# The last stage of a four-layer graph network: one PSUM bank per chunk, twice x as an early float32 product, the last norm on two engines

## The chip, the core and the metric

The kernel runs on one core of a Trainium2 chip. The core has five engines that run their own instruction streams and meet only at semaphores: TensorE (matrix products, into PSUM), VectorE, ScalarE, GpSimd and SyncE (which issues DMAs). The time is the device time of one execution in microseconds. Before the change it was 1755.76 us (median of 3 runs, 1755.16 to 1755.86).

## The reference

Node states x (3125 nodes, 128 features) go through four layers of a graph network over 100,000 edges, each followed by `x = layernorm(x + layer(x))`. The change concerns the end of the fourth, a graph isomorphism layer:

```python
def _L3_gnn_ref(x, edge_index, W, b, gamma, beta, gin_eps):
    agg = jax.ops.segment_sum(x[src], dst, num_segments=x.shape[0])
    h = (1.0 + gin_eps[0]) * x + agg
    h = h @ W.T + b
    mean = jnp.mean(h, axis=0)                     # over the nodes
    var = jnp.mean(jnp.square(h - mean), axis=0)
    h = gamma * (h - mean) * jax.lax.rsqrt(var + BN_EPS) + beta
    return jax.nn.relu(h) + x
...
x = _layernorm(x + _L3_gnn_ref(x, ...), axis=-1)   # so: layernorm(relu(bn(z)) + 2 x)
return x
```

The batch norm needs the statistics of all nodes, so nothing of Relu or the last norm can start until the last node's z = h W^T + b is known. Behind it come Relu, the sum with 2x, and a norm over the 128 features of each node.

## The kernel before

The nodes stand in 25 tiles of 128 (the last holds 53), in `CHUNKS` of four tiles (seven chunks, the last of one tile) or in `PAIR`s of eight (three pairs and one tile). The edges are turned into a dense adjacency matrix `adj` in SBUF, with which every layer's sum over neighbours is a matrix product; x is split for it into three bf16 parts, `parts[0..2]`, whose sum is x in float32. A long loop over the edges (layer 1) fills most of the time; layers 2 and 3 follow. The order of the work is written out by hand for every engine, and each engine runs its list in order.

The end of layer 3: for each chunk u, `l3_terms` sums into PSUM bank u (the tail into bank 7), VectorE copies the sum to SBUF (`l3_out`, into `acc`), TensorE multiplies it by the weight back into the same bank (`l3_linear`, signals `gin_ready`), ScalarE adds the bias and writes z, with features on partitions, to `agg_all` (`gin_rows`, signals `gin_out`), and VectorE takes batch statistics of it (`zt_stats`). `agg_all` and `xn`, which holds x in float32 by rows, are the same 3200 columns of the arena: from here on x exists only as its three parts. VectorE then forms scale and bias of the batch norm as two columns of `cols`, with ScalarE's square root (`root`) in between. At `phase_end(eng, 8)` each engine drains, adds one to `phase_ends` and waits for all five.

The last stage runs over the four groups of `PAIR`. ScalarE applies Relu with scale and bias to eight tiles of z at once (`bn_relu`). TensorE, for every tile, adds twice x into PSUM as three bf16 products of `parts` with `ident_h` (an identity that VectorE doubles just then) and adds the Relu's tile, turned by a float32 product with `ident_f` (`fin_ready`); it has two banks for a group and two groups in flight, so from the third group on it waits for `out_ready`. VectorE's `layernorm` takes statistics of each of the eight rows of tiles, combines them, lets ScalarE take the roots, forms the reciprocal and normalises eight times, from PSUM into `xn`. SyncE stores a group when it is done. The branch `If_ne(flag, 0)` serves graphs that don't fit the fast layout; it isn't taken here.

Of the kernel before, what the change touches and what calls it, by code (L numbers as in the profile page):

```python
# [23 lines left out]
ALU = mybir.AluOpType  # L24
ACT = mybir.ActivationFunctionType

P = 128
N = 3125
E = 100000
D = 128  # L30
# [13 lines left out]
CH = 4  # L44
# [26 lines left out]
def build(nc, t, out, x1_d, xa_d, xb_d, table_d, late_d):  # L71
    ctx = ExitStack()
    with ctx:
# [3 lines left out]
        def sem(name):  # L77
            return ctx.enter_context(nc.semaphore(name))
# [111 lines left out]
        agg_all = arena[:, 4800:8000]  # L190


        eps_i = late[:, 0:P]
        node2 = [late[:, P + 512 * u:P + 512 * (u + 1)].rearrange("p (j d) -> p j d", d=D) for u in range(2)]


# [25 lines left out]
        cnt_ready = sem("cnt_ready")  # L222
        adj_written = sem("adj_written")
        lin_base = {0: 0, 1: NC, 2: 3 * NC}
        zero_ready = sem("zero_ready")
        deg_ready = sem("deg_ready")
        words_moved = sem("words_moved")
        c1_sum_ready = sem("c1_sum_ready")
# [55 lines left out]
        fin_ready = sem("fin_ready")  # L284
        out_ready = sem("out_ready")
        twice_ready = sem("twice_ready")
        out_stored = sem("out_stored")
        off_ready = sem("off_ready")
        off_t = sem("off_t")
# [103 lines left out]
        def dst_bank(u):  # L393
            return ps[:, u, :] if u < NC - 1 else ps[:, 7, P:2 * P]
# [64 lines left out]
        def _(sp):  # L459
# [188 lines left out]
            with sp.Else():  # L648
# [7 lines left out]
                sp.wait_ge(xb_ready, NC)  # L656
                l2_affine()
                sp.sem_inc(phase_ends, 1)
            phase_end(sp, 8)

            for g, (k0, nt) in enumerate(PAIR):
                sp.wait_ge(out_ready, g + 1)
                if nt == 2 * CH:
                    sp.dma_start(out[k0 * P:(k0 + nt) * P, :].rearrange("(k p) d -> p k d", p=P),
                                 xn[:, k0:k0 + nt, :]).then_inc(out_stored, 16)
                else:
                    sp.dma_start(out[k0 * P:N, :], xn[0:TAIL, k0, :]).then_inc(out_stored, 16)
# [4 lines left out]
        def _(pool):  # L672
# [100 lines left out]
            with pool.Else():  # L773
# [3 lines left out]
                    pool.tensor_tensor(xn[:, k0:k0 + nt, :], xn[:, k0:k0 + nt, :], over(beta_b, nt), ALU.add  # L777
                                       ).then_inc(xb_ready, 1)
                pool.sem_inc(phase_ends, 1)
            phase_end(pool, 8)  # L780


        @block.tensor
        def _(pe):
# [447 lines left out]
            with pe.If_ne(flag, 0):  # L1232
                pe.wait_ge(update_loaded, 48)
                pe.wait_ge(bn_loaded, 16)
                for c in range(NC):
                    update(c)
                transposed_weight(loads[7], 16)
                scan(pe, X2, scan_tile)
                layer(2, gcn, summed, peeled=2)
                phase_end(pe, 7)  # L1240
                transposed_weight(loads[9], 80)
                scan(pe, X3, scan_tile)
                layer(3, gin, summed, peeled=1)
            with pe.Else():
                for c, bank in ((NC - 2, 6), (NC - 1, 3)):
                    update_tiles(c, range(CHUNKS[c][1]), bank, w_b)
                behind = late_sums(EARLY - 1)
                for u in behind:
                    l2_terms(EARLY - 1, u, True, False)
                weight_t(loads[7], 16, 0)  # L1250
                weight_t(loads[9], 80, 1)
                pe.wait_ge(low_ready, 2 * NC + NC - 1)
                for u in range(NC):
                    if u == 2:
                        pe.wait_ge(wt_ready, 2)
                    if u == 3:
                        pe.wait_ge(lin_used, 3 * NC)
                    l2_terms(NC - 2, u, u not in behind, False)
                pe.wait_ge(low_ready, 3 * NC)
                for u in ORDER:  # L1260
                    l2_terms(NC - 1, u, False, True)
                l2_linear(ORDER[0])
                l2_linear(ORDER[1])
                pe.wait_ge(eps_ready, 1)
                for n, c in enumerate(ORDER[:-1]):
                    pe.wait_ge(low_ready, 3 * NC + n + 1)
                    for u in ORDER:
                        if n == 0:
                            pe.wait_ge(agg_out, 2 * NC + AT[u] + 1)
                        l3_terms(c, u)  # L1270
                    if n + 2 < NC:
                        l2_linear(ORDER[n + 2])
                pe.wait_ge(low_ready, 4 * NC)
                pe.wait_ge(wt_ready, 2)
                for u in range(NC):
                    l3_terms(ORDER[-1], u)
                    if u:
                        l3_linear(u - 1)
                l3_linear(NC - 1)
                pe.sem_inc(phase_ends, 1)  # L1280
            phase_end(pe, 8)

            pe.wait_ge(twice_ready, 1)
            for g, (k0, nt) in enumerate(PAIR):
                pe.wait_ge(bn_relu, g + 1)
                if g >= 2:
                    pe.wait_ge(out_ready, g - 1)
                for j in range(nt):
                    k = k0 + j
                    o = ps[:, 2 * (g % 2) + j // CH, (j % CH) * D:(j % CH + 1) * D]  # L1290
                    for q in range(3):
                        pe.matmul(o, ident_h[:, :], parts[q][:, k, :], start=(q == 0), stop=False)
                    last = pe.matmul(o, agg_all[:, k * P:(k + 1) * P], ident_f[:, :], start=False, stop=True)
                last.then_inc(fin_ready, 1)


        @block.scalar
        def _(act):
# [1 line left out]
                out = words(k0, k1).bitcast(F32)  # L1300
                act.activation(out, cols[:, 6:7].broadcast_to([P, (k1 - k0) * NP // 2]), ACT.Copy)

            act.wait_ge(zero_ready, 1)
            zero(3, 8)
            for n in range(8):
                half, a = n // 4, n % 4
# [280 lines left out]

            def gin_chunk(c, k0, nt):
                act.wait_ge(gin_ready, c + 1)
                act.activation(agg_all[:, k0 * P:(k0 + nt) * P], ps[:, 4, 0:nt * P], ACT.Identity,  # L1590
                               bias=cols[:, 0:1]).then_inc(gin_out, 1)

            def two_roots(c, k0, nt):
# [54 lines left out]
            def gin_rows(u):  # L1648
                k0, nt = CHUNKS[u]
                act.wait_ge(gin_ready, u + 1)  # L1650
                act.activation(agg_all[:, k0 * P:(k0 + nt) * P], dst_bank(u), ACT.Identity,
                               bias=cols[:, 0:1]).then_inc(gin_out, 1)

            with act.Else():
# [22 lines left out]
                root(1)  # L1677
                act.sem_inc(phase_ends, 1)
            assert roots[0] == after
            phase_end(act, 8)  # L1680

            for k0, nt in PAIR:
                act.activation(agg_all[:, k0 * P:(k0 + nt) * P], agg_all[:, k0 * P:(k0 + nt) * P], ACT.Relu,
                               bias=cols[:, 6:7], scale=cols[:, 5:6]).then_inc(bn_relu, 1)
            for k0, nt in PAIR:
                root(nt)


        @block.vector
        def _(dve):  # L1690
            own = Count(dve, v_own)

            dve.memset(cols[:, 7:8], EPS)
            dve.memset(cols[:, 6:7], 0.0).then_inc(zero_ready, 1)
            own.add(dve.memset(off[:, :], 0.0))
            dve.wait_ge(loads[0], 48)
            own.add(dve.tensor_scalar(hi_i[0:GRP, :], raw_src[0:GRP, :], 7, None, ALU.arith_shift_right))
# [498 lines left out]
            def zt_stats(c):  # L2196
                k0, nt = CHUNKS[c]
                dve.wait_ge(gin_out, c + 1)
                w = nt * P if nt == CH else TAIL
                own.add(dve.bn_stats(stats[:, c, :], agg_all[:, k0 * P:k0 * P + w]))  # L2200

            def gcn_all(add, rows, ahead):
                added = [0]
# [18 lines left out]
            with dve.If_ne(flag, 0):  # L2222
# [17 lines left out]
                for c in range(NC):  # L2240
                    add_self(3, c, gin_ready, 0)
                    zt_stats(c)
                own.wait()
                dve.sem_inc(var_ready, ROOTS)
                roots[0] += ROOTS
                dve.sem_inc(v_own, OWN_MORE)
# [70 lines left out]
            with dve.Else():  # L2317
# [12 lines left out]
                for c in ORDER:  # L2330
# [14 lines left out]
                    if c == ORDER[0]:  # L2345
                        add_sums(ORDER[5])
                        add_sums(ORDER[6])
                dve.wait_ge(loads[9], 80)
                for u in range(NC):
                    l3_out(u)  # L2350
                    if u:
                        zt_stats(u - 1)
# [10 lines left out]
            own.wait()  # L2363
            own.add(dve.tensor_tensor(rstd[:, 1:2], cols[:, 5:6], mv[:, 0, 0:1], ALU.mult))
            own.wait()
            dve.tensor_tensor(cols[:, 6:7], cols[:, 2:3], rstd[:, 1:2], ALU.subtract)
            phase_end(dve, 8)

            dve.tensor_scalar(ident_h[:, :], ident_h[:, :], 2.0, None, ALU.mult).then_inc(twice_ready, 1)
            for g, (k0, nt) in enumerate(PAIR):  # L2370
                dve.wait_ge(fin_ready, g + 1)
                b = 2 * (g % 2)
                layernorm(ps[:, b:b + 2, :].rearrange("p a (j d) -> p (a j) d", d=D), xn[:, k0:k0 + nt, :], nt, done=out_ready)


_INS = ["x", "src", "dst", "edge_attr_64", "L0_gnn_W_self1", "L0_gnn_W_neigh1", "L0_gnn_b1", "L0_gnn_W_self2",
# [26 lines left out]
```

## Time and profile before

| | us |
|---|---|
| median of the runs shown | 1755.76 |
| the profiled execution, its own time | 1752.44 |
| its span, first to last instruction | 1750.3 |
| TensorE busy in the span | 1468.5 |
| VectorE busy | 760.0 |
| ScalarE busy | 668.9 |
| last product of layer 3 ends, from the span's start | 1718.46 |
| last store issued | 1746.60 |

The profiled execution's own time contains a little beyond the span. Times in the rows below count from the span's start. Busy shares over the whole span say nothing of the last stage, which is 2% of it; it has to be read from its own chain and timeline. PE is TensorE's matmul unit and PEld its weight load, DVE is VectorE, ACT ScalarE, SPq the DMA queue of SyncE. A float32 product appears as two instructions of PE.

### The profile page before, as it was taken

Reading aid. Unit: us, or ns where it says so; the run is one execution under the profiler, and the core shown is the slowest. Engines: PE = TensorE matmul, PEld = TensorE weight load, DVE = VectorE, ACT = ScalarE, POOL = GpSimd, SP = SyncE. Lnnn points to the kernel's source line nnn. Section 1 sums busy time; section 2 is a strip of 40 time slices with the busy share of each in tenths; the row PEclk is TensorE's granted clock in tenths of the full one; section 3 lists DMA queues with packets and bytes.
Section 4 is the critical chain, followed back from the end, with each engine's and each line's share of the span. In section 5 each row is a group of like instructions: output and inputs, shape, how many; then the busy total and the mean of one; then the engine's idle time right before and its main releaser. Section 6 shows DMA issues by size and latency. Waiting matters only on the chain.

```text
span 1750.3 us, 31633 instructions
## 1 busy us (share of the span) xinstructions
PE 1468.5 (84%) x9759; PEld 1049.2 (60%) x9872; DVE 760.0 (43%) x2792; ACT 668.9 (38%) x1236; POOL 784.7 (45%) x819
## 2 busy tenths in 40 slices
PE   1789999969986877888888888889888988957996
PEld 1346666644545766676666666667666766634554
DVE  6997888622333322233334334323433343235445
ACT  3765555520002433344335334434433453321111
POOL 4300000000003777777777777777777777710000
PEclk9999999989997999989999999999999999969998
DMA  2000000001005333333333333333333333300001
GB/s 78 1 0 1 2 1 1 2 25 38 0 0 158 98 82 82 82 86 83 82 80 87 83 82 80 88 79 85 84 82 82 83 86 82 74 11 1 1 1 38
DMA packets 158697, 95.81 MB, mean 55 GB/s; under 512 B 120584, under 2 KB 143879, under 8 KB 158607
## 3 DMA queue, kind: packets, MB, share of 16 engines
q0 software_dynamic: 25088, 51.43, 11.4%
q1 hardware_dynamic: 133519, 43.21, 10.0%
q8 instruction: 53, 0.87, 0.2%
q14 instruction: 37, 0.30, 0.1%
HBM read 87.24 MB, written 7.32 MB: 54 GB/s over the span
## 4 chain that ended last, share of the span: by engine, by line
PE 31%; DMA 11%; POOL 9%; issue 8%; DVE 5%; ACT 2%; DVEq 2%; SPq 1%; POOLq 0%; ACTq 0%
DMA arena<-x_w1a,idx 9%; POOL arena L751 9%; PE ps L1077 6%; PE ps L1217 6%; PE ps L1086 5%; PE ps L1070 4%; PE ps L1058 3%; PE ps L1066 3%; PE ps L1127 1%; PE ps L1201 1%; DVE arena L1986 1%; DVEq L328 1%; DMA arena<-in_edge_attr 1%; DVE idx L1955 1%; ACT arena L1490 1%
## 5 line engine op out<-in xcount | busy, mean ns | idle before, releaser
L751 POOL DMA_INDIRECT arena<-x_w1a,idx x784 | 742.3, 947 | 692.2 <-issue 651.9
L1480 ACT ACTIVATE arena<-ps 88x512 f32<-88x512 f32 x196 | 116.3, 594 | 478.9 <-PE ps L1058 473.4
L1086 PEld LDWEIGHTS ps<-arena 128*128 128x128 f32 x1568 | 208.4, 195 | 111.5 <-issue 74.0
L1066 PE MATMUL ps<-ident_f,arena 128*128 128x128 f32 x784 | 132.6, 294 | 110.4 <-DMA arena<-x_w1a,idx 109.7
L1986 DVE TENSOR_TENSOR arena<-ps,bias_b 128x512 f32<-128x512 f32 x196 | 135.6, 692 | 204.6 <-PE ps L1077 204.6
L1981 DVE TENSOR_TENSOR arena<-win_i,late 128x96 f32<-128x96 f32 x196 | 51.4, 262 | 391.5 <-PE ps L1086 380.7
L1077 PE MATMUL ps<-w_c,arena 128*128 128x128 f32 x1568 | 221.3, 287 | 0.0
L1319 ACT ACTIVATE adj<-ps 128x300 f32 x392 | 172.5, 450 | 125.2 <-PE ps L815 118.1
L1070 PE MATMUL ps<-arena 88*128 88x512 f32 x392 | 208.3, 613 | 3.7 <-ACT arena L1480 3.7
L1077 PEld LDWEIGHTS ps<-w_c,arena 128*128 128x128 f32 x1568 | 204.4, 203 | 0.2
L1086 PE MATMUL ps<-arena 128*128 128x24 f32 x1568 | 197.0, 264 | 5.3 <-ACT arena L1490 2.9
L810 PE MATMUL ps<-arena 128*128 128x300 bf16 x784 | 168.2, 297 | 34.4 <-DVE arena L1754 30.4
L1754 DVE TENSOR_SCALAR arena<-late,arena 128x300 bf16<-128x300 int16 x784 | 191.6, 309 | 0.0
L1066 PEld LDWEIGHTS ps<-ident_f,arena 128*128 128x128 f32 x784 | 91.1, 148 | 163.9 <-DMA arena<-x_w1a,idx 158.7
L1486 ACT ACTIVATE arena<-ps,cols 128x512 f32<-128x512 f32 x196 | 134.7, 687 | 73.0 <-PE ps L1077 73.0
L1058 PE MATMUL ps<-ident_f,arena 128*88 128x128 f32 x784 | 128.1, 289 | 21.8 <-DMA arena<-in_edge_attr 14.6
L810 PEld LDWEIGHTS ps<-arena 128*128 128x128 bf16 x784 | 83.5, 115 | 91.6 <-DVE arena L1754 38.9
L827 PE MATMUL ps<-adj,arena 128*128 128x512 bf16 (+1 forms) x498 | 134.5, 357 | 0.5 <-issue 0.2
L1490 ACT ACTIVATE arena<-arena 128x512 f32<-128x512 f32 x196 | 123.4, 630 | 10.5 <-DVE arena L1986 3.3
L815 PE MATMUL ps<-adj,ident_h 128*128 x392 | 124.0, 316 | 0.8 <-ACT adj L1319 0.2
L959 PE MATMUL ps<-adj,arena 128*128 (+1 forms) x513 | 104.0, 362 | 16.6 <-DVE arena L1813 16.1
L1217 PE MATMUL ps<-adj,arena 128*128 128x512 bf16 (+1 forms) x513 | 108.2, 363 | 8.8 <-DVE arena L2309 4.8
(187 smaller groups left out, 1447.0 us busy)
## 6 DMA issues: line engine op xcount, KB each, us to landing
arena<-in_edge_attr SPq DMA_DIRECT2D x196, 128.0 KB, 2.5
arena<-x_w1a,idx POOLq DMA_INDIRECT x784
arena<-x_w1b SPq DMA_DIRECT2D x196, 12.0 KB
x_spill<-arena SPq DMA_DIRECT2D x1, 1600.0 KB, 7.2
x_w1a<-arena SPq DMA_DIRECT2D x6, 256.0 KB, 2.3
x_w1b<-arena SPq DMA_DIRECT2D x6, 256.0 KB, 2.6
arena<-x_spill SPq DMA_DIRECT2D x6, 256.0 KB, 2.8
out_x<-arena SPq DMA_DIRECT2D x3, 512.0 KB
```

Of the source, the lines that this page charges most:

```text
L751: pool.indirect_dma_start(out=z_e[v][:, j * D:(j + 1) * D], out_offset=None, in_=xa_d[:, :], in_offset=bass.IndirectOffsetOnAxis(ap=idx[:, ...
L810: last = pe.matmul(ps[:, bank, 0:NT * WIN_A], oh_src[v][:, :, j], oh_dst[v][:, j, :], start=(j == 2 * h), stop=False)
L1058: last = pe.transpose(ps[0:KE, 0, j * P:(j + 1) * P], ec[v % 2][:, j, :], ident_f[:, :])
L1066: pe.matmul(z_t[:, j * P:(j + 1) * P], z_e[v][:, j * P:(j + 1) * P], ident_f[:, :], is_transpose=True, start=(j == 0), stop=False)
L1070: pe.matmul(z_t, w_e[v % 2][0:KE, :], ec_t[0:KE, :], start=False, stop=True).then_inc(z_ready[v], 1)
L1077: last = pe.matmul(ps[:, 5, j * P:(j + 1) * P], h_t[:, j * P:(j + 1) * P], w_c[:, :], start=True, stop=True)
L1086: last = pe.matmul(ps[:, WIN_BANK[v % 2], 0:WIN], msg[:, j * P:(j + 1) * P], oh_e[v][:, j, :], start=(j == 0), stop=(j == J - 1))
L1217: last = pe.matmul(dst_bank(u), parts[q][:, k, :], adj[:, k, k0 * P:(k0 + nt) * P], start=((k, q) == (NT - 1, 0)), stop=(u != NC - 2 and ( ...
L1319: act.activation(adj[:, :, bass.ds(b, WIN_A)], ps[:, q % 4, 0:NT * WIN_A].rearrange("p (k w) -> p k w", w=WIN_A), ACT.Copy).then_inc(adj_w ...
L1490: act.activation(msg, msg, ACT.Relu).then_inc(msg_ready[v], 1)
L1754: last = dve.tensor_scalar(oh_dst[v][:, j, :], iota_c, comb[:, bass.ds(s, 1), j], None, ALU.is_equal)
L1986: dve.tensor_tensor(msg.rearrange("p (j d) -> p j d", d=D), bank(5, J), over(bias_b, J), ALU.add).then_inc(m_sum[v], 1)
```

## The change

- z goes to `z_t`, which is `acc`, the place of the sums it is made from, and not over `xn`: x stays whole in float32.
- Twice x is one float32 product for a chunk, 512 columns of `xn` against `twice_i`, a doubled identity that VectorE now makes ahead of its layer-3 copies. It opens the accumulation in PSUM bank c of chunk c. Four chunks' products stand ahead of the first Relu's tiles in TensorE's order, the others between the chunks.
- Relu goes by chunks of four tiles, and TensorE adds each chunk's four tiles to its bank. With a bank for every chunk, nothing in TensorE's list waits for `out_ready`.
- The join of all engines, `phase_end(eng, 8)`, is gone. ScalarE waits for VectorE's factors by `cols_ready`.
- VectorE takes statistics by chunk. In a group of eight tiles it normalises the first four and ScalarE the other four, with the negated scaled mean `nbias` as bias. VectorE's combining of the next group's statistics waits until both halves are done, since they read the same `mv`, `rstd` and `nbias`.

```diff
+        z_t = acc
+        twice_i = late[:, 9 * P:10 * P]
...
-            phase_end(sp, 8)
-
             for g, (k0, nt) in enumerate(PAIR):
-                sp.wait_ge(out_ready, g + 1)
+                sp.wait_ge(out_ready, min(2 * g + 2, NC))
...
-            phase_end(pe, 8)
-
             pe.wait_ge(twice_ready, 1)
-            for g, (k0, nt) in enumerate(PAIR):
-                pe.wait_ge(bn_relu, g + 1)
-                if g >= 2:
-                    pe.wait_ge(out_ready, g - 1)
+
+            def twice_x(c):
+                k0, nt = CHUNKS[c]
+                pe.wait_ge(gin_out, c + 1)
+                pe.matmul(ps[:, c, 0:nt * D], twice_i, xn[:, k0:k0 + nt, :].rearrange("p k d -> p (k d)"),
+                          start=True, stop=False)
+
+            def add_bn(c):
+                k0, nt = CHUNKS[c]
+                pe.wait_ge(bn_relu, c + 1)
                 for j in range(nt):
-                    k = k0 + j
-                    o = ps[:, 2 * (g % 2) + j // CH, (j % CH) * D:(j % CH + 1) * D]
-                    for q in range(3):
-                        pe.matmul(o, ident_h[:, :], parts[q][:, k, :], start=(q == 0), stop=False)
-                    last = pe.matmul(o, agg_all[:, k * P:(k + 1) * P], ident_f[:, :], start=False, stop=True)
+                    last = pe.matmul(ps[:, c, j * D:(j + 1) * D], z_t[:, (k0 + j) * P:(k0 + j + 1) * P], ident_f[:, :],
+                                     start=False, stop=(j == nt - 1))
                 last.then_inc(fin_ready, 1)
+
+            for c in range(4):
+                twice_x(c)
+            for c in range(NC):
+                add_bn(c)
+                if c + 4 < NC:
+                    twice_x(c + 4)
...
-            phase_end(act, 8)
-
-            for k0, nt in PAIR:
-                act.activation(agg_all[:, k0 * P:(k0 + nt) * P], agg_all[:, k0 * P:(k0 + nt) * P], ACT.Relu,
+            act.wait_ge(cols_ready, 2)
+            for k0, nt in CHUNKS:
+                act.activation(z_t[:, k0 * P:(k0 + nt) * P], z_t[:, k0 * P:(k0 + nt) * P], ACT.Relu,
                                bias=cols[:, 6:7], scale=cols[:, 5:6]).then_inc(bn_relu, 1)
-            for k0, nt in PAIR:
+            for g, (k0, nt) in enumerate(PAIR):
                 root(nt)
+                if nt == 2 * CH:
+                    act.wait_ge(fin_norm, g + 1)
+                    for j in range(CH, nt):
+                        last = act.activation(xn[:, k0 + j, :], ps[:, 2 * g + 1, (j - CH) * D:(j - CH + 1) * D], ACT.Identity,
+                                              scale=rstd[:, j:j + 1], bias=nbias[:, j:j + 1])
+                    last.then_inc(out_ready, 1)
...
                 dve.wait_ge(loads[9], 80)
+                dve.tensor_scalar(twice_i, ident_f[:, :], 2.0, None, ALU.mult).then_inc(twice_ready, 1)
                 for u in range(NC):
                     l3_out(u)
...
-            phase_end(dve, 8)
-
-            dve.tensor_scalar(ident_h[:, :], ident_h[:, :], 2.0, None, ALU.mult).then_inc(twice_ready, 1)
...
             for g, (k0, nt) in enumerate(PAIR):
-                dve.wait_ge(fin_ready, g + 1)
-                b = 2 * (g % 2)
-                layernorm(ps[:, b:b + 2, :].rearrange("p a (j d) -> p (a j) d", d=D), xn[:, k0:k0 + nt, :], nt, done=out_ready)
+                halves = [(2 * g, CH), (2 * g + 1, CH)] if nt == 2 * CH else [(2 * g, nt)]
+                for c, n in halves:
+                    dve.wait_ge(fin_ready, c + 1)
+                    for j in range(n):
+                        own.add(dve.bn_stats(stats[:, CH * (c - 2 * g) + j, :], rows_of(c, n)[:, j, :]))
+                own.wait()
+                if g:
+                    dve.wait_ge(out_ready, 2 * g)
+                for j in range(nt):
+                    last = dve.bn_aggr(mv[:, j, :], stats[:, j, :])
+                last.then_inc(var_ready, 1)
...
+                if nt == 2 * CH:
+                    dve.scalar_tensor_tensor(out=nbias[:, 0:nt], in0=mv[:, 0:nt, 0], scalar=-1.0, in1=rstd[:, 0:nt],
+                                             op0=ALU.mult, op1=ALU.mult).then_inc(fin_norm, 1)
+                c, n = halves[0]
+                for j in range(n):
+                    last = dve.tensor_scalar(xn[:, k0 + j, :], rows_of(c, n)[:, j, :], mv[:, j, 0:1], rstd[:, j:j + 1],
+                                             ALU.subtract, ALU.mult)
```

How the lists of the engines read before and after, with the semaphores that each row waits for. TensorE, from the last product of layer 3 on (`ps` is PSUM, `arena` holds z, x and its parts). Before:

```order
L1229 MATMUL ps<-arena,w_a 128x128 [waits agg_out]
L1244 UNCONDITIONAL_BRANCH
L1292 MATMUL ps<-arena,ident_h 128x128 [waits bn_relu,twice_ready,phase_ends]
L1292 MATMUL ps<-arena,ident_h 128x128 x2
L1293 MATMUL ps<-ident_f,arena 128x128
L1292 MATMUL ps<-arena,ident_h 128x128 x3
L1293 MATMUL ps<-ident_f,arena 128x128
```

In the changed kernel, at the same place (`late` holds the doubled identity):

```order
L1229 MATMUL ps<-arena,w_a 128x128 [waits agg_out]
L1245 UNCONDITIONAL_BRANCH
L1287 MATMUL ps<-arena,late 128x512 [waits gin_out,twice_ready]
L1287 MATMUL ps<-arena,late 128x512 [waits gin_out] x3
L1294 MATMUL ps<-ident_f,arena 128x128 [waits bn_relu]
L1294 MATMUL ps<-ident_f,arena 128x128 x3
L1287 MATMUL ps<-arena,late 128x512 [waits gin_out]
L1294 MATMUL ps<-ident_f,arena 128x128 [waits bn_relu]
L1294 MATMUL ps<-ident_f,arena 128x128 x3
```

The first instruction that needs the Relu was the first of the stage; now it is the fifth, behind four products that need only x.

VectorE, one group of eight tiles of the last norm. Before (the second group):

```order
L1838 BN_STATS stats<-ps 128x6 [waits fin_ready,v_own]
L1838 BN_STATS stats<-ps 128x6 x7
L1841 BN_AGGR mv<-stats 128x2 [waits v_own]
L1841 BN_AGGR mv<-stats 128x2 x7
L1845 RECIPROCAL rstd<-std 128x8 [waits std_ready]
L1848 TENSOR_SCALAR arena<-ps,mv,rstd 128x128 [waits v_own]
L1848 TENSOR_SCALAR arena<-ps,mv,rstd 128x128 x7
```

In the changed kernel, the same group:

```order
L2392 BN_STATS stats<-ps 128x6 [waits fin_ready]
L2392 BN_STATS stats<-ps 128x6 x3
L2392 BN_STATS stats<-ps 128x6 [waits fin_ready]
L2392 BN_STATS stats<-ps 128x6 x3
L2397 BN_AGGR mv<-stats 128x2 [waits out_ready,v_own]
L2397 BN_AGGR mv<-stats 128x2 x7
L2401 RECIPROCAL rstd<-std 128x8 [waits std_ready]
L2404 SCALAR_TENSOR_TENSOR nbias<-mv,rstd 128x8 [waits v_own]
L2408 TENSOR_SCALAR arena<-ps,mv,rstd 128x128 x4
```

Four of the eight normalising instructions have left VectorE; the combining has a new wait for the other engine's half of the group before.

ScalarE, from the root of the batch norm on. Before:

```order
L1405 ACTIVATE std<-mv,cols 128x1 [waits var_ready]
L1654 UNCONDITIONAL_BRANCH
L1683 ACTIVATE arena<-arena,cols 128x1024 [waits phase_ends]
L1683 ACTIVATE arena<-arena,cols 128x1024 x2
L1683 ACTIVATE arena<-arena,cols 128x128
L1405 ACTIVATE std<-mv,cols 128x8 [waits var_ready] x3
L1405 ACTIVATE std<-mv,cols 128x1 [waits var_ready]
```

In the changed kernel:

```order
L1414 ACTIVATE std<-mv,cols 128x1 [waits var_ready]
L1663 UNCONDITIONAL_BRANCH
L1691 ACTIVATE arena<-arena,cols 128x512 [waits cols_ready]
L1691 ACTIVATE arena<-arena,cols 128x512 x5
L1691 ACTIVATE arena<-arena,cols 128x128
L1414 ACTIVATE std<-mv,cols 128x8 [waits var_ready]
L1698 ACTIVATE arena<-ps,nbias,rstd 128x128 [waits fin_norm]
L1698 ACTIVATE arena<-ps,nbias,rstd 128x128 x3
L1414 ACTIVATE std<-mv,cols 128x8 [waits var_ready]
```

Between the roots stand now four normalising instructions a group, read from PSUM.

## Rows read from the trace of the kernel before

**Rows 1.** Chain that ended last: start us, us, what (x instructions)
```profile
1704.18 0.86 PE ps L1229 x2
...
1720.85 0.16 DVE cols L2366
...
1721.08 1.25 ACT arena L1683
...
1722.46 0.48 PE ps L1292 x3
1722.94 0.53 PE ps L1293 x2
...
1728.15 0.29 PE ps L1293 x2
1728.46 1.70 DVE stats L1838 x8
```

**Rows 2.** Timeline of the last norm: start us, us, engine, line, instruction, [idle before]
```profile
1733.99 1.68 DVE L1838 BATCH_NORM_STATS2 stats<-ps 128x6 f32<-128x128 f32 x8
...
1735.70 0.64 DVE L1841 BATCH_NORM_AGGREGATE mv<-stats 128x2 f32<-128x6 f32 x8
...
1736.38 0.30 ACT L1405 ACTIVATE std<-mv,cols 128x8 f32<-128x8 f32 x1 [5.22 <-DVE mv L1841]
...
1736.71 0.20 DVE L1845 RECIPROCAL rstd<-std 128x8 f32<-128x8 f32 x1 [0.37 <-ACT std L1405]
...
1736.95 2.64 DVE L1848 TENSOR_SCALAR arena<-ps,mv,rstd 128x128 f32<-128x128 f32 x8
...
1739.57 1.68 DVE L1838 BATCH_NORM_STATS2 stats<-ps 128x6 f32<-128x128 f32 x8
...
1745.42 0.18 DVE L1841 BATCH_NORM_AGGREGATE mv<-stats 128x2 f32<-128x6 f32 x1
...
1746.60 0.26 SPq L667 DMA_DIRECT2D out_x<-arena  x1
```

**Rows 3.** Waits of SyncE's queue: who for whom, us in total, times, longest
```profile
SPq L73 <- DMA out_x<-arena: 3.0, 1, 3.0
```

**Rows 4.** Timeline of TensorE, layers 2 and 3
```profile
1677.40 1.05 PE L1181 MATMUL ps<-w_c,arena 128*128 128x128 f32 x8
...
1716.78 1.68 PE L1229 MATMUL ps<-arena,w_a 128*128 128x512 f32 x4
```

**Rows 5.** Timeline of a layer-2 norm that both engines write
```profile
1684.80 0.30 ACT L1405 ACTIVATE std<-mv,cols 128x4 f32<-128x4 f32 x1 [3.53 <-DVE mv L2003]
1685.13 0.18 DVE L2288 RECIPROCAL rstd<-std 128x4 f32<-128x4 f32 x1 [0.36 <-ACT std L1405]
...
1685.42 1.11 DVE L2296 TENSOR_SCALAR arena<-late,mv,rstd 128x128 f32<-128x128 f32 x4
1685.54 1.65 ACT L1639 ACTIVATE arena<-late,nbias,rstd 128x128 bf16<-128x128 f32 x4 [0.44 <-DVE nbias L2290]
```

**Rows 6.** ScalarE by form: shapes, count | busy us, mean ns
```profile
L1683 ACT ACTIVATE arena<-arena,cols 128x1024 f32<-128x1024 f32 x3 | 3.5, 1231 | 0.8 <-DVEq L306 0.8
...
L1301 ACT ACT_TABLE_LOAD x1 | 1.3, 1283 | 0.6 <-PEq L2388 0.6
...
L1683 ACT ACTIVATE arena<-arena,cols 128x128 f32<-128x128 f32 x1 | 0.5, 478 | 0.0
```

**Rows 7.** Stretches: us, PE, PEld, DVE, ACT, POOL busy, granted clock, DMA
```profile
1720.00:1721.00 1.00, 0.00 (x0) 0.00 (x0) 0.64 (x4) 0.23 (x1) 0.00 (x0) 0.69 0.00 0
1723.00:1724.00 1.00, 1.00 (x7) 0.94 (x7) 0.00 (x0) 1.00 (x2) 0.00 (x0) 0.50 0.00 0
...
1008.00:1010.00 2.00, 0.59 (x6) 0.40 (x5) 0.85 (x3) 1.42 (x3) 1.46 (x2) 1.00 0.54 119
```

**Rows 8.** Timeline of TensorE in the edge loop
```profile
1009.77 0.44 PE L1066 MATMUL ps<-ident_f,arena 128*128 128x128 f32 x2 [1.41 <-DMA arena<-x_w1a,idx]
```

**Rows 9.** Timeline of VectorE at the first layer-3 copy
```profile
1698.25 0.69 DVE L2315 COPY arena<-ps 128x512 f32<-128x512 f32 x1 [8.94 <-PE ps L1217]
```

More of the change, by code:

```diff
@@ L224, in build @@
         lin_base = {0: 0, 1: NC, 2: 3 * NC}
-        zero_ready = sem("zero_ready")
+        cols_ready = sem("cols_ready")
         deg_ready = sem("deg_ready")
@@ L286, in build @@
         twice_ready = sem("twice_ready")
+        fin_norm = sem("fin_norm")
         out_stored = sem("out_stored")
@@ L779, in _ @@
                 pool.sem_inc(phase_ends, 1)
-            phase_end(pool, 8)
         @block.tensor
@@ L1243, in _ @@
                 layer(3, gin, summed, peeled=1)
+                pe.wait_ge(gin_out, NC)
             with pe.Else():
@@ L1301, in zero @@
                 act.activation(out, cols[:, 6:7].broadcast_to([P, (k1 - k0) * NP // 2]), ACT.Copy)
-            act.wait_ge(zero_ready, 1)
+            act.wait_ge(cols_ready, 1)
             zero(3, 8)
@@ L1589, in gin_chunk @@
                 act.wait_ge(gin_ready, c + 1)
-                act.activation(agg_all[:, k0 * P:(k0 + nt) * P], ps[:, 4, 0:nt * P], ACT.Identity,
+                act.activation(z_t[:, k0 * P:(k0 + nt) * P], ps[:, 4, 0:nt * P], ACT.Identity,
                                bias=cols[:, 0:1]).then_inc(gin_out, 1)
@@ L1650, in gin_rows @@
                 act.wait_ge(gin_ready, u + 1)
-                act.activation(agg_all[:, k0 * P:(k0 + nt) * P], dst_bank(u), ACT.Identity,
+                act.activation(z_t[:, k0 * P:(k0 + nt) * P], dst_bank(u), ACT.Identity,
                                bias=cols[:, 0:1]).then_inc(gin_out, 1)
@@ L1693, in _ @@
             dve.memset(cols[:, 7:8], EPS)
-            dve.memset(cols[:, 6:7], 0.0).then_inc(zero_ready, 1)
+            dve.memset(cols[:, 6:7], 0.0).then_inc(cols_ready, 1)
             own.add(dve.memset(off[:, :], 0.0))
@@ L2199, in zt_stats @@
                 w = nt * P if nt == CH else TAIL
-                own.add(dve.bn_stats(stats[:, c, :], agg_all[:, k0 * P:k0 * P + w]))
+                own.add(dve.bn_stats(stats[:, c, :], z_t[:, k0 * P:k0 * P + w]))
             def gcn_all(add, rows, ahead):
@@ L2348, in _ @@
                 dve.wait_ge(loads[9], 80)
+                dve.tensor_scalar(twice_i, ident_f[:, :], 2.0, None, ALU.mult).then_inc(twice_ready, 1)
                 for u in range(NC):
@@ L2365, in _, with rows_of @@
             own.wait()
-            dve.tensor_tensor(cols[:, 6:7], cols[:, 2:3], rstd[:, 1:2], ALU.subtract)
-            phase_end(dve, 8)
-            dve.tensor_scalar(ident_h[:, :], ident_h[:, :], 2.0, None, ALU.mult).then_inc(twice_ready, 1)
+            dve.tensor_tensor(cols[:, 6:7], cols[:, 2:3], rstd[:, 1:2], ALU.subtract).then_inc(cols_ready, 1)
+            def rows_of(c, nt):
+                return ps[:, c, 0:nt * D].rearrange("p (j d) -> p j d", d=D)
             for g, (k0, nt) in enumerate(PAIR):
-                dve.wait_ge(fin_ready, g + 1)
-                b = 2 * (g % 2)
-                layernorm(ps[:, b:b + 2, :].rearrange("p a (j d) -> p (a j) d", d=D), xn[:, k0:k0 + nt, :], nt, done=out_ready)
+                halves = [(2 * g, CH), (2 * g + 1, CH)] if nt == 2 * CH else [(2 * g, nt)]
[9 more added lines that the diff above has]
+                last.then_inc(var_ready, 1)
+                roots[0] += 1
+                dve.wait_ge(std_ready, roots[0])
+                own.add(dve.reciprocal(rstd[:, 0:nt], std[:, 0:nt]))
+                own.wait()
+                if nt == 2 * CH:
[5 more added lines that the diff above has]
+                                             ALU.subtract, ALU.mult)
+                    if j < n - 1:
+                        own.add(last)
+                last.then_inc(out_ready, 1)
 _INS = ["x", "src", "dst", "edge_attr_64", "L0_gnn_W_self1", "L0_gnn_W_neigh1", "L0_gnn_b1", "L0_gnn_W_self2",
```

## The prediction

> **What bounds the kernel now.** I read the chain that ended last from its end backwards [rows 1], then the timeline of VectorE, ScalarE and SyncE's queue over the last 17 us [rows 2], and then prices from other places. All that the change touches lies behind the last layer-3 matrix product, so only the last 32 us count; in every engine's order the instructions ahead are the same, but for one small VectorE instruction. The reader is to see three pieces. First TensorE stops: its last product of layer 3 ends at 1718.46 [rows 4], ScalarE and VectorE finish the batch-norm factors (last one 1720.85 + 0.16 = 1721.01), Relu of eight tiles runs 1721.08 to 1722.33, and only then does TensorE start, 1722.46 [rows 1]. Second, TensorE is the bound: eight tiles, the first ones at half pace, until 1728.44, and VectorE starts its statistics at 1728.46 [rows 1]. Third, VectorE is the bound: groups of eight tiles begin at 1728.46, 1733.99 and 1739.57, some 5.55 us each, and TensorE is far ahead or waits for PSUM. The tail tile's statistics are combined at 1745.42 and its store leaves at 1746.60 [rows 2]. What follows is that store's 3.0 us [rows 3] and the end of the program. The store is the same afterwards, so the end moves as its issue moves.
>
> **The drain and join of all engines, removed.** The Relu starts 0.07 us behind the last factor (1721.01 to 1721.08) [rows 1], and an ordinary handover from VectorE to ScalarE takes 0.04 (1735.70 + 0.64 to 1736.38) [rows 2]. I take 0; the bounds are a gain of 0.1 and nothing lost, since no other engine was late there. The Relu stays at 1721.08.
>
> **Relu in chunks of four tiles.** A row of 1024 elements takes 1.231 us and one of 128 takes 0.478 [rows 6], so 0.84 ns an element: 512 take 0.478 + 384 x 0.84 ns = 0.80. Chunk 0 is ready at 1721.88 and TensorE, 0.13 behind (1721.08 + 1.25 = 1722.33, to 1722.46), starts on it at 1722.02. Later chunks follow every 0.7 us, faster than TensorE eats them.
>
> **Two times x, early.** The twelve bf16 products of a chunk (three parts, four tiles) become one float32 product 512 wide. The row of that shape takes 0.86 us (first line of [rows 1]). Four of the seven are placed ahead of the Relu: they need banks 0 to 3 empty and the doubled identity, both long since there. From 1718.46 they run 4 x 0.86 = 3.44, to 1721.90, 0.12 before the first Relu chunk can be used. They lie wholly in the time in which TensorE used to stand still. Between stands only the branch out of the layer-3 code. If TensorE is late behind it, every tenth beyond 0.12 costs a tenth; no row shows TensorE starting work there, since it used to wait. Bounds: 0, and 3.44 - 0.12 = 3.3 (all four behind the Relu). I take 0, since everything that the four need is there at 1718.46. The doubling of the identity now stands ahead of VectorE's first layer-3 copy, which waits 8.94 us for TensorE [rows 9]; cost 0.
>
> **What is left behind the Relu.** Four tiles of z^T against the float32 identity: the nearest row is four float32 tiles, each with its own stationary operand, at 1.05 us [rows 4]. Chunk 0: 1722.02 to 1723.07; the early product of chunk 4, queued between, to 1723.93; chunk 1 to 1724.98. VectorE no longer waits for a pair: it takes chunk 0 while TensorE works on chunk 1, so only chunk 1's four statistics remain, half of 1.70 [rows 1]. Combining starts at 1724.98 + 0.02 + 0.86 = 1725.86, where before it was 1728.46 + 1.71 = 1730.17. This is the first gain, 4.3 us. It contains the clock. Before, TensorE had stood still since 1718.46, the granted clock read 0.69 from 1720 to 1721 and 0.50 from 1723 to 1724 [rows 7]: it was at 1.2 GHz, and a float32 tile took 0.53 instead of 0.29 [rows 1]. Now TensorE is busy without a hole that matters. In the edge loop a stop of 1.41 us [rows 8] left the stretch around it at 1.00 [rows 7], so I take 2.4 GHz throughout.
>
> **The last norm, shared.** From combining to the first normalised row takes 1.25 us (1735.70 to 1736.95); the new negated mean adds 0.05, since with it the rows begin 0.29 behind the reciprocal (1685.13 to 1685.42) [rows 5] and without it 0.24 (1736.71 to 1736.95) [rows 2]. Then VectorE has four rows, not eight: half of 2.64, 1.32. A group costs VectorE 1.71 + 1.30 + 1.31 = 4.32, against 5.58 (1733.99 to 1739.57). From 1725.86 it is through with the three groups at 1728.47, 1732.79 and 1737.11. TensorE delivers chunk 3 at about 1728.2 and chunk 5 at 1730.3, ahead of need.
>
> **ScalarE's half.** The row to compare is four 128-wide rows with scale and bias, 1.65 us, begun 0.12 behind VectorE's rows [rows 5]; there the input is in SBUF, here in PSUM. Below, I put 1.65; above, four unoverlapped rows of 0.48 [rows 6], 1.92. I take 1.65, since the nearest row overlaps. The Trainium skill's "PSUM: Partial Sum Buffer" (its part ahead of "PSUM: the matmul accumulator") says that ScalarE and VectorE read PSUM in parallel at full bandwidth while they keep to different banks, which would leave the sum as it is; no run so far shows the pair. What is queued behind: VectorE's combining of the next group waits for this half, but only 1.31 + 1.71 = 3.02 us after its own rows begin, while ScalarE ends 0.12 + 1.65 = 1.77 after; there are 1.25 us to spare. Only the third group's half is in the open: it ends at 1735.80 + 1.77 = 1737.57. The tail tile's combining waits for it, 1737.61, where VectorE alone could have begun at about 1737.44. From there to the tail's store the row is 1.18 (1745.42 to 1746.60) [rows 2]: 1738.79.
>
> **Sum.** 1746.60 - 1738.79 = 7.8 us. By pieces: 4.3 before the first combining, then 1.2 to 1.26 for each of three groups, less 0.17 for the wait at the tail. The profiled execution took 1752.44 us (span 1750.3), 3.3 below the median of the runs shown, 1755.76; the piece has the same length in both, so 1755.76 - 7.8 = 1748.0. A change of this kernel under 0.2%, 3.5 us, cannot be told from none.
>
> **Rivals.**
> *The clock is low all the same.* For it: the last stage began at 1.2 GHz before, behind the stop from 1718.46 to 1722.46. Against: that stop is filled. If it is low until chunk 1 is out, that takes 2.10 + 1.72 + 2.10 instead of 1.05 + 0.86 + 1.05, 2.96 more: gain 4.9, 1750.9. If it stays low to the end, TensorE becomes the bound, chunk 5 comes at 1738.6, ScalarE's last half ends 5.0 later than above: gain 2.8, 1752.9.
> *The early products aren't early.* TensorE starts them late behind its branch. For it: the step over the branch is nowhere shown with work behind it. Against: nothing is waited for. Begun 1.6 us late: 1749.5. Wholly behind the Relu: 1751.3.
> *ScalarE changes its table between root and rows.* In the trace the root of a group at 1684.80 is followed by scaled rows at 1685.54 with no load between [rows 5], and a load, where there is one, takes 1283 ns [rows 6]. If one stood there, ScalarE would start 1.28 - 0.44 = 0.84 later, hidden twice and open once: 1748.8. The Trainium skill's "ScalarE: Activation LUTs" ("What ACT_TABLE_LOAD costs") gives 2.66 us with its drain for every switch to another set, an estimate of 1752.1 by that; the trace shows no such switch between these two functions.
> *Slower: ScalarE's half becomes the bound.* Place: the wait of VectorE's combining for ScalarE's rows. Were its PSUM rows held up by VectorE's reads so that four take x, two groups lose x - 2.9 and the last loses x - 1.65. Nothing is gained at x = 5.1, 1.27 us a row, three times the row's 0.41; slower by 0.2% needs 1.56 a row, 1759.3. Against: VectorE's own reads of a group last 1.3 us, so that even waiting them out gives x near 3, not 6.
>
> **How the numbers follow.** Forecast as summed, own range 1747.2 to 1749.0: 0.78. Clock low for a while 0.07, to the end 0.03. Early products late 0.06 (a little over half of it near 1749.5). Table 0.01. Slower 0.03. The remaining 0.02 is a gain eaten elsewhere, no change. Range 1746.9 to 1751.0: below it is the forecast with 0.5 us for the scatter of the runs (0.7 in all) and the drain's tenth; above it reaches over the half-low clock and the late products. Faster by over 0.2%, under 1752.2: 0.78 + 0.07 + 0.06 + 0.01 = 0.92; within: 0.05; slower: 0.03.
>
> **What would show it.** TensorE's row of four products 512 wide starts near 1718.5 and ends near 1721.9; the granted clock reads 1.00 from 1712 to 1730; VectorE's first statistics begin near 1723.1, with a stop of about one microsecond between the halves of group one and none later; groups repeat every 4.3 us; ScalarE's rows take 1.65 a group and hold up only the tail; the third large store leaves near 1737.6, the tail's near 1738.8. It is wrong if the clock drops, if ScalarE's rows pass 2.9 us, or if TensorE begins the early products after 1719.

## The result

The changed kernel took 1746.22 us (median of 4 runs, 1745.71 to 1747.23) against 1755.46 for the kernel before beside it (4 runs, 1752.97 to 1755.86): ratio 0.995, 95% interval 0.9934 to 0.9966, so 9.2 us faster. The forecast was 1748.0, the range 1746.9 to 1751.0; the time lies 0.7 us under the range. Timed again later the two took 1745.02 and 1753.06, ratio 0.9951 (0.9937 to 0.9965), 8.0 us.

The profiled execution of the changed kernel took 1746.03 us, its span 1743.7. Times in all rows below count from the start of the span of their own trace. To compare last stages I measure from one event in both kernels, the start of ScalarE's copy of the last two chunks of z (the row with 0.97 us), to the issue of the tail's store. Before, the first of these is this row of the timeline (columns as in [rows 2]):

```profile
1717.89 0.97 ACT L1651 ACTIVATE arena<-ps,cols 128x512 f32<-128x512 f32 x2 [0.90 <-PE ps L1229]
...
1730.18 0.64 DVE L1841 BATCH_NORM_AGGREGATE mv<-stats 128x2 f32<-128x6 f32 x8
```

With the store at 1746.60 [rows 2] that makes 28.71 us; the second row is the first combining of statistics (the 128x6 of eight tiles into `mv`), 12.29 us behind the copy. After, the timeline of the same stretch:

```profile
1719.14 0.97 ACT L1660 ACTIVATE arena<-ps,cols 128x512 f32<-128x512 f32 x2 [0.90 <-PE ps L1229]
...
1722.30 4.72 ACT L1691 ACTIVATE arena<-arena,cols 128x512 f32<-128x512 f32 x7 [0.81 <-DVE cols L2382]
...
1727.04 0.64 DVE L2397 BATCH_NORM_AGGREGATE mv<-stats 128x2 f32<-128x6 f32 x8
...
1728.37 1.37 DVE L2408 TENSOR_SCALAR arena<-ps,mv,rstd 128x128 f32<-128x128 f32 x4
1728.49 1.51 ACT L1698 ACTIVATE arena<-ps,nbias,rstd 128x128 f32<-128x128 f32 x4 [0.47 <-DVE nbias L2404]
1729.65 1.67 DVE L2392 BATCH_NORM_STATS2 stats<-ps 128x6 f32<-128x128 f32 x8
...
1731.35 0.64 DVE L2397 BATCH_NORM_AGGREGATE mv<-stats 128x2 f32<-128x6 f32 x8
...
1735.67 0.64 DVE L2397 BATCH_NORM_AGGREGATE mv<-stats 128x2 f32<-128x6 f32 x8
...
1737.12 1.51 ACT L1698 ACTIVATE arena<-ps,nbias,rstd 128x128 f32<-128x128 f32 x4 [0.47 <-DVE nbias L2404]
...
1738.72 0.18 DVE L2397 BATCH_NORM_AGGREGATE mv<-stats 128x2 f32<-128x6 f32 x1 [0.16 <-ACT arena L1698]
...
1739.91 0.26 SPq L668 DMA_DIRECT2D out_x<-arena  x1
```

1739.91 - 1719.14 = 20.77 us, 7.94 less; the sum had 7.81. The first combining starts 7.90 us behind the copy. The combining instructions of the three groups stand 4.31 and 4.32 us apart, where a group took 5.58 before [rows 2]. ScalarE's four rows take 1.51 and end inside VectorE's next statistics; only the tail's combining waits for them, 0.16 us.

The start of the stage, in the chain that ended last (columns as in [rows 1]):

```profile
1719.21 0.49 PE ps L1229 x2
1719.70 3.44 PE ps L1287 x8
1723.14 0.02 issue
1723.17 1.16 PE ps L1294 x8
1724.33 0.86 PE ps L1287 x2
1725.19 0.91 PE ps L1294 x8
```

The four early products (L1287, eight instructions) run from 1719.70 to 1723.14, in what was a stop of four microseconds [rows 1, 4]. They stand on this chain themselves: the Relu's first chunk comes at the same moment, and TensorE goes on without a stop. Its clock, by stretches (columns as in [rows 7]):

```profile
1720.00:1721.00 1.00, 1.00 (x4) 0.52 (x3) 0.85 (x3) 0.11 (x1) 0.00 (x0) 1.00 0.00 0
...
1722.00:1724.00 2.00, 1.98 (x10) 1.02 (x9) 0.23 (x2) 1.70 (x3) 0.00 (x0) 1.00 0.00 0
```

1.00 in these and in every other stretch from 1712 to 1730, which is 2.4 GHz, where 0.69 and 0.50 stood before [rows 7].

So the trace shows the stage as the sum had it. The whole times don't follow it as closely: the two profiled executions differ by 6.4 us (1752.44 and 1746.03), since the stage began 1.25 us later in the second, and the medians by 9.2 the first time and by 8.0 the second. For that the sum has no term.

### The profile page after: what moved, and what is told of

Same layout as the page of the kernel before. It is cut to its first block, busy times and chain, and to the rows that moved or that the text cites. A ratio compares the mean times of both kernels' runs of the same rounds, so it can differ in the third digit from the quotient of the medians.

```text
span 1743.7 us, 31506 instructions
## 1 busy us (share of the span) xinstructions
PE 1457.8 (84%) x9698; PEld 1037.2 (59%) x9811; DVE 754.7 (43%) x2783; ACT 674.6 (39%) x1251; POOL 784.8 (45%) x819
## 4 chain that ended last, share of the span: by engine, by line
PE 30%; DMA 12%; POOL 9%; issue 8%; DVE 5%; ACT 3%; DVEq 1%; SPq 1%; POOLq 0%; ACTq 0%
DMA arena<-x_w1a,idx 10%; POOL arena L752 9%; PE ps L1077 6%; PE ps L1217 6%; PE ps L1086 5%; PE ps L1070 5%; PE ps L1058 3%; PE ps L1066 3%; PE ps L1201 1%; DVE arena L2000 1%; DMA arena<-in_edge_attr 1%; PE ps L1127 1%; DVE idx L1969 1%; DVEq L331 1%; ACT arena L1499 1%
```

## The experiments

The first four ran on one chip, the other four on another, each beside runs of the kernel before (medians 1753.06, 18 runs, and 1753.83, 17 runs). "Last stage" is the stretch defined above, from each one's own trace.

| | last stage, us | median, us | ratio to before, 95% |
|---|---|---|---|
| kernel before, copy | 29.34 | 1752.80 | 1.000 (0.999 to 1.0009) |
| changed kernel, copy | 20.77 | 1745.02 | 0.9951 (0.9937 to 0.9965) |
| without ScalarE's half | 24.24 | 1749.15 | 0.9975 (0.9963 to 0.9988) |
| late products of x | 24.21 | 1747.66 | 0.9967 (0.9955 to 0.9979) |
| late products, filled stop | 21.62 | 1747.22 | 0.996 (0.9944 to 0.9975) |
| before, filled stop | 26.46 | 1749.59 | 0.9981 (0.9972 to 0.9989) |
| changed, with the join | 26.42 | 1748.26 | 0.9967 (0.9954 to 0.998) |
| changed, other order | 19.96 | 1743.00 | 0.9944 (0.9931 to 0.9956) |

**The kernel before, copied, and the changed kernel, copied.** No edit.

> The kernel before, unchanged, timed against itself on one chip beside the changed kernel. Theory A (the traced 7.9 us of the last stage are the whole gain; the rest of the measured 9.2 is the scatter of the kernel before, whose profiled execution took 1752.4 and whose runs took 1753.0 to 1755.9): ratio 1.000, single runs spread over 2 to 3 us, the way from the last layer-3 product to the tail's store 28.1 us again, and the spread lies ahead of it. Theory B (the change saves 1 to 3 us outside the last stage that the one trace of before did not show): every run of it near 1755.5.

> The changed kernel once more, more rounds. Theory A: 7.9 us below the kernel before on the same chip, ratio 0.9955; last layer-3 product to tail's store 20.2 us. Theory B: 9.2 us or more below, ratio 0.9948 or less.

Single executions of the copy took 1750.69 to 1758.15 us, and those of the kernel before beside it 1750.68 to 1757.35: one kernel, over 7 us apart, most of them below 1755. That is a miss of the expectation, which had 2 to 3 us. The changed kernel's spread over 1742.59 to 1747.36, its last stage 20.77 again. Its gain, 8.0 by medians, is A's 7.9 and not B's 9.2, but its ratio, 0.9951, lies midway between the two that were expected, and the ratio's interval (6.1 to 11.0 us) would hold both. What speaks against B is that the copy of the kernel before doesn't stay near 1755.5. But the copy's last stage is not 28.1 plus 0.6 (28.71): it is 29.34.

```profile
1718.69 0.97 ACT L1651 ACTIVATE arena<-ps,cols 128x512 f32<-128x512 f32 x2 [0.90 <-PE ps L1229]
...
1723.26 0.48 PE L1292 MATMUL ps<-arena,ident_h 128*128 128x128 bf16 x3 [4.01 <-ACT arena L1683]
...
1729.79 1.68 DVE L1838 BATCH_NORM_STATS2 stats<-ps 128x6 f32<-128x128 f32 x8 [7.67 <-PE ps L1293]
...
1748.03 0.26 SPq L667 DMA_DIRECT2D out_x<-arena  x1
```

TensorE's first group took from 1723.26 to 1729.79, 6.5 us, where it took 6.0 before [rows 1]: more of it ran at 1.2 GHz. The granted clock was still 0.50 from 1728 to 1729, 4.7 to 5.7 us behind the group's start; in the first trace it was 0.90 from 1727 to 1728, 4.5 to 5.5 us behind. So the spread does not lie ahead of the last stage alone: 0.6 us of it are inside the old stage, whose length differs from execution to execution, and by the second trace the change saves 8.57 us. The changed kernel's two traces agree to a hundredth.

**Without ScalarE's half.**

```diff
-                    for j in range(CH, nt):
-                        last = act.activation(xn[:, k0 + j, :], ps[:, 2 * g + 1, ...], ACT.Identity,
-                                              scale=rstd[:, j:j + 1], bias=nbias[:, j:j + 1])
...
-                c, n = halves[0]
-                for j in range(n):
+                for c, n in halves:
+                    for j in range(n):
```

> The changed kernel without ScalarE's half: VectorE normalises all eight tiles of a group, and the negated mean isn't formed. If the sharing is worth what the sum says: a group goes from 4.32 back to 5.58 less the 0.05 of the negated mean, 3 x 1.21 = 3.6, less 0.2 for the tail that no longer waits for ScalarE: 3.4 us slower than the changed kernel. Rival (the two engines slow each other's PSUM reads, so the sharing gives little): under 1.5 us slower.

3.47 us longer by the stage, 4.1 by medians. The combining instructions are 5.5 us apart again:

```profile
1718.92 0.97 ACT L1660 ACTIVATE arena<-ps,cols 128x512 f32<-128x512 f32 x2 [0.90 <-PE ps L1229]
...
1726.82 0.64 DVE L2391 BATCH_NORM_AGGREGATE mv<-stats 128x2 f32<-128x6 f32 x8
...
1732.34 0.64 DVE L2391 BATCH_NORM_AGGREGATE mv<-stats 128x2 f32<-128x6 f32 x8
...
1743.16 0.26 SPq L668 DMA_DIRECT2D out_x<-arena  x1
```

The sharing is worth what the sum said, and the rival, under 1.5 us because the two engines hold up each other's reads, falls.

**Late products of x.**

```diff
-            for c in range(4):
-                twice_x(c)
             for c in range(NC):
+                pe.wait_ge(bn_relu, c + 1)
+                twice_x(c)
                 add_bn(c)
-                if c + 4 < NC:
-                    twice_x(c + 4)
```

> The changed kernel with each chunk's product of x only behind that chunk's Relu, so that TensorE stands still between layer 3 and the Relu as before. If the early products are worth their place and the clock: TensorE works at 1.2 GHz, chunk 1 is out after 1.72 + 2.10 + 1.72 + 2.10 = 7.6 us instead of 2.96: 4.7 us slower, 3 if the clock comes back halfway. Rival (the clock has no part in it): only one product of 0.86 more lies ahead of chunk 1: 0.9 us slower.

3.44 us longer by the stage (2.6 by medians), between the two values named. The timeline shows why:

```profile
1719.16 0.97 ACT L1658 ACTIVATE arena<-ps,cols 128x512 f32<-128x512 f32 x2 [0.90 <-PE ps L1229]
...
1723.24 2.04 PE L1287 MATMUL ps<-arena,late 128*128 128x512 f32 x2 [3.51 <-issue]
1725.07 1.92 PE L1294 MATMUL ps<-ident_f,arena 128*128 128x128 f32 x8
1726.78 1.87 PE L1287 MATMUL ps<-arena,late 128*128 128x512 f32 x2
...
1728.49 1.06 PE L1294 MATMUL ps<-ident_f,arena 128*128 128x128 f32 x8
...
1743.37 0.26 SPq L668 DMA_DIRECT2D out_x<-arena  x1
```

and the stretch from 1723 to 1728 (columns as in [rows 7])

```profile
1723.00:1728.00 5.00, 4.76 (x12) 3.22 (x13) 0.89 (x4) 4.05 (x7) 0.00 (x0) 0.50 0.00 0
```

Behind a stop of 3.51 us, the first product of x, the four Relu tiles and the second product start 1.83 and 1.71 us apart, and the second chunk's tiles 1.71 later; in the changed kernel's chain such a product takes 0.86 and four tiles 0.91. The granted clock there was 0.50, which is 1.2 GHz. At 1728.49 the pace is back, which is the halfway that the expectation named.

**Late products, filled stop.** The same, with four products whose result is not used in the stop.

```diff
+            for c in range(4):
+                pe.wait_ge(gin_out, c + 1)
+                pe.matmul(ps[:, 6, :], twice_i, xn[:, CH * c:CH * c + CH, :]..., start=True, stop=True)
             for c in range(NC):
                 pe.wait_ge(bn_relu, c + 1)
                 twice_x(c)
```

> As the run with the late products of x, but with four products of the same size, whose result is not used, in the time in which TensorE stood still. The last stage, from ScalarE's copy of the last two chunks of z to the tail's store, took 20.77 us in the changed kernel and 24.21 with the late products. If the clock made most of the difference: granted clock 1.00 throughout and 20.77 + 0.9 = 21.6 us, the one product that still lies ahead of chunk 1. Rival (the place of the products made it): 24 us again.

```profile
1721.48 0.97 ACT L1662 ACTIVATE arena<-ps,cols 128x512 f32<-128x512 f32 x2 [0.90 <-PE ps L1229]
...
1725.51 1.12 PE L1287 MATMUL ps<-arena,late 128*128 128x512 f32 x2
1726.47 1.05 PE L1294 MATMUL ps<-ident_f,arena 128*128 128x128 f32 x8
...
1743.10 0.26 SPq L668 DMA_DIRECT2D out_x<-arena  x1
```

The product and the tiles behind it now start 0.96 us apart, and the stretch from 1716 to 1736 (columns as in [rows 7]) shows the clock at 1.00:

```profile
1716.00:1736.00 20.00, 19.86 (x103) 12.51 (x102) 10.77 (x52) 9.02 (x18) 0.00 (x0) 1.00 0.09 26
```

The stage is 21.62. Of the 3.44 us that the late products cost, 2.59 are the clock and 0.85 the one product more ahead of chunk 1.

**The kernel before, filled stop.**

```diff
                 l3_linear(NC - 1)
+                for c in range(3):
+                    pe.matmul(ps[:, 6, :], ident_f[:, :], acc[:, 512 * c:512 * c + 512], start=True, stop=True)
```

> The kernel before with three products 512 wide, whose result is not used, behind the last layer-3 product, 2.6 us in the time in which TensorE stood still. If the clock was a good half of the first gain of 4.3 us: TensorE keeps 2.4 GHz, the first group takes 8 x 0.44 = 3.5 us instead of 6.0, the last stage 26.3 instead of 28.7 us (29.3 in the second trace of the kernel before). Rival (the clock falls all the same in what is left of the stop, 1.4 us): 28.7 or more.

```profile
1717.12 0.97 ACT L1653 ACTIVATE arena<-ps,cols 128x512 f32<-128x512 f32 x2 [0.90 <-PE ps L1229]
...
1721.70 0.33 PE L1294 MATMUL ps<-arena,ident_h 128*128 128x128 bf16 x3 [1.44 <-ACT arena L1685]
...
1725.45 1.68 DVE L1840 BATCH_NORM_STATS2 stats<-ps 128x6 f32<-128x128 f32 x8 [4.90 <-PE ps L1295]
...
1743.58 0.26 SPq L667 DMA_DIRECT2D out_x<-arena  x1
```

The microsecond in which TensorE goes on behind the stop that is left (columns as in [rows 7]):

```profile
1721.00:1722.00 1.00, 0.30 (x4) 0.33 (x5) 0.00 (x0) 1.00 (x2) 0.00 (x0) 1.00 0.04 8
```

26.46: the first group takes 3.75 us of TensorE instead of 6.0. Three useless products make the kernel before 0.19% faster (4.2 us by medians, 2.3 to 2.9 by the stages); behind the stop of 1.44 us that is left the granted clock is 1.00, up to 1728. From there to the changed kernel without ScalarE's half, 24.24, are 2.22 us more: a shorter list of TensorE behind the Relu, the Relu and the statistics by chunks, no join. With the 2.25 of the clock (28.71 to 26.46) and the 3.47 of the sharing they make up the 7.94; no run takes those 2.22 apart.

**The changed kernel with the join.**

```diff
+            phase_end(pe, 8)
             pe.wait_ge(twice_ready, 1)
```

and the same on the other four engines.

> The changed kernel with the drain and join of all engines put back where it stood. The prediction priced the join alone at 0 to 0.1 us. If it is worth nothing: the last stage 20.8 to 20.9 us. Rival (the join is what kept the early products from being early): they start only behind the batch-norm factors, at 1.2 GHz for some 4.5 us, chunk 1 is out 3.5 to 5.6 us later, the last stage 24.3 to 26.4 us.

```profile
1716.22 0.97 ACT L1663 ACTIVATE arena<-ps,cols 128x512 f32<-128x512 f32 x2 [0.90 <-PE ps L1231]
...
1719.44 4.72 ACT L1695 ACTIVATE arena<-arena,cols 128x512 f32<-128x512 f32 x7 [0.88 <-DVEq L309]
1719.45 6.72 PE L1290 MATMUL ps<-arena,late 128*128 128x512 f32 x8 [2.67 <-DVEq L309]
...
1726.01 1.05 PE L1297 MATMUL ps<-ident_f,arena 128*128 128x128 f32 x8
...
1742.64 0.26 SPq L669 DMA_DIRECT2D out_x<-arena  x1
```

and one of the stretches (columns as in [rows 7])

```profile
1720.00:1721.00 1.00, 1.00 (x2) 0.34 (x1) 0.00 (x0) 1.00 (x3) 0.00 (x0) 0.50 0.03 8
```

The Relu starts 0.88 us behind ScalarE's last work with the join (its idle time in brackets), and 0.81 without, in the changed kernel: the join as such costs 0.07. But the four products start with the Relu instead of 2.6 us earlier (1719.70 against 1722.30 in the changed kernel), and at 1.2 GHz, the granted clock being 0.50, they take 6.6 us instead of 3.44. The stage is 5.65 us longer, over two thirds of the gain. By the ratios of the times, taken on different chips (0.9967 and 0.9951), it is 2.8 us and their intervals overlap, so the size rests on the trace. The join stood ahead of the products in TensorE's list; with the products put ahead of the join nothing was run.

**The changed kernel, other order.** The chain of the changed kernel has a product of x (1724.33, 0.86) between the Relu tiles of chunks 0 and 1.

```diff
             for c in range(NC):
+                if c >= 4:
+                    twice_x(c)
                 add_bn(c)
-                if c + 4 < NC:
-                    twice_x(c + 4)
```

> The changed kernel with the products of x for chunks 4 to 6 moved behind the Relu tiles of chunk 3, so that chunk 1 follows chunk 0 at once. Chunk 1 is out 0.86 us earlier, and VectorE, which waited 0.86 us for it, goes straight on: the last stage 19.9 instead of 20.77 us. Rival (VectorE is bound by something else by then): 20.8. The time itself would move by less than its runs scatter.

```profile
1715.01 0.97 ACT L1660 ACTIVATE arena<-ps,cols 128x512 f32<-128x512 f32 x2 [0.90 <-PE ps L1229]
...
1719.04 3.84 PE L1294 MATMUL ps<-ident_f,arena 128*128 128x128 f32 x32
1720.23 1.78 DVE L2392 BATCH_NORM_STATS2 stats<-ps 128x6 f32<-128x128 f32 x8 [2.10 <-PE ps L1294]
...
1734.97 0.26 SPq L668 DMA_DIRECT2D out_x<-arena  x1
```

VectorE takes its eight statistics in one go. 19.96, 0.81 less than the changed kernel. By the stage it beats both kernels; by the times it can't be told from the changed kernel: the two ratios, 0.9944 and 0.9951, lie well within each other's intervals.

**Where the scatter lies.** In the ten traces the last stage begins between 1715.01 and 1721.48, though nothing ahead of it was changed but one VectorE instruction. The two ends and the kernel before, at the last gather of the edge loop (timeline of GpSimd): first the changed kernel in the other order, whose stage begins at 1715.01, then the kernel before, 1717.89, then the late products with the filled stop, 1721.48.

```profile
1525.08 0.95 POOL L752 DMA_INDIRECT arena<-x_w1a,idx  x1 [0.30 <-issue]
```

```profile
1527.38 0.94 POOL L751 DMA_INDIRECT arena<-x_w1a,idx  x1 [0.30 <-issue]
```

```profile
1530.08 0.94 POOL L752 DMA_INDIRECT arena<-x_w1a,idx  x1 [0.30 <-issue]
```

5.0 of the 6.5 us are there by the end of the edge loop. From there to the stage the ten traces differ by another 2.5 us (189.9 to 192.4). Why one execution's loop is longer than another's was not tried and stays open.

## Why the prediction was wrong

By its own steps:

- **The join: 0, bounds 0 to 0.1.** Right for the join alone (0.07). What the step didn't say is that the early products could not be early with it where it stood; with it there, 5.65 us of the gain go by the trace.
- **Relu in chunks, four early products: no cost.** Right. They end at 1723.14, and the first Relu tile starts at 1723.17; the margin of 0.12 was used up, but not passed. By the letter one of the signs of being wrong came: they began at 1719.70, after 1719. But the last layer-3 product ended only there, the whole stage lying 1.25 us later in this execution, so they were not late.
- **First gain 4.3, the clock in it.** Right: 4.39 (12.29 from the copy to the first combining before, 7.90 after). The clock's part, which the prediction did not give apart, is 2.3 in the kernel before (28.71 to 26.46; 2.9 from its second trace) and 2.6 in the changed one.
- **A group 4.32, ScalarE's four rows 1.65, 0.17 lost at the tail.** Right: 4.31 and 4.32, 1.51, 0.16. ScalarE's rows cost a little less than the row that they were compared with, so the lower of the two bounds was the better one, and not low enough. That row reads SBUF and writes bf16 [rows 5], these read PSUM and write float32; which of the two makes the difference was not tried. The sum did not hang on it: they ended well before anything but the tail waited for them.
- **Sum 7.8 us.** 7.94 by the traces, 8.6 against the second trace of the kernel before, in which more of TensorE's first group ran at 1.2 GHz. That the sum comes as near as 0.13 is in part luck of the trace it was read from.
- **"The piece has the same length in both, so 1755.76 - 7.8 = 1748.0", and a range with "0.5 us for the scatter of the runs (0.7 in all)".** This step failed: the level of the base and the room for scatter, not the gain. Three runs between 1755.16 and 1755.86 were read as the level and the spread of the kernel, though the profiled execution, 1752.44, already stood 3.3 below their median; it was set aside with one sentence. The twenty-nine executions of the second comparison lie between 1750.68 and 1758.15, with medians of 1752.8 and 1753.1, and only five of them reach 1755.16; against that spread the three lie close together and high. The gain of 7.8 from 1753.06 gives 1745.3; measured beside it, 1745.02. In the first comparison the kernel before came out at 1755.5 and the changed one at 1746.2, 9.2 less, with an interval of 6.0 to 11.6: medians of four runs each could not have carried a bound only 1.1 under the forecast. Nor do the terms named give that bound: 1748.0 less 0.5 to 0.7 and less 0.1 is 1747.2 to 1747.4, not 1746.9. How the 1.3 us beyond the stage divide between chance, another level of the kernel before on that occasion and a first group that ran at 1.2 GHz for more of its length, four runs of each can't tell; this stays open.

Of the rivals, the low clock, the late products, the table between root and rows and ScalarE's half as the bound did not come; no ACT_TABLE_LOAD stands in the stage. The second rival's price, 1751.3, had all four products behind the Relu at 2.4 GHz; the run with the join shows that they would not have had that clock.

## What to carry to other kernels

Here a stop of TensorE cost more than its length: behind four microseconds it worked at half clock, 2.3 to 2.9 us in the kernel before. So look for work that is needed anyway to fill such a stop, and try even work that isn't. A join that costs next to nothing as a wait (0.07 us) can still forbid the order that brings the gain (5.65 us by the trace), so price it together with what it blocks. And before a gain of a few microseconds is laid on a base, ask every execution in sight how far the base itself moves: the profiled one was a fourth beside the three, and said so.

## What the runs showed of the hardware

- TensorE's granted clock was at 0.50 behind the stop of four microseconds in the kernel before [rows 7] and at 1.00 behind one of 1.44 us at the same place. Later in the kernel before, behind a stop of 2.24 us for PSUM ahead of its third group, it was 0.50 again (1734 to 1737), off the chain that ended last. The first group of eight tiles took 6.0 us and 6.5 us in two traces with the first, 3.75 with the second.
- ScalarE's four rows of 128 elements with scale and bias took 1.51 us from PSUM, beside VectorE's four from another bank in 1.37; before, four from SBUF with bf16 output took ScalarE 1.65 [rows 5], and eight from PSUM on VectorE alone 2.64 [rows 2]. The Trainium skill's "PSUM — Partial Sum Buffer", in its part ahead of "PSUM: the matmul accumulator", has the two engines read PSUM in parallel at full bandwidth from different banks; the trace agrees, 1.37 being half of 2.64 and a twentieth of a microsecond.
